# Query and key stacks of three narrow attentions: six copies in DRAM and one load each, in place of three parts and six loads

## What is computed

```python
Q = (queries @ W_q.T).reshape(b, lq, H, DH).transpose(2, 0, 1, 3)
K = (keys @ W_k.T).reshape(b, lk, H, DH).transpose(2, 0, 1, 3)
V = (keys @ W_v.T).reshape(b, lk, H, DH).transpose(2, 0, 1, 3)
scores = jnp.einsum('hbqd,hbkd->hbqk', Q, K) / jnp.sqrt(jnp.float32(DH))
scores = jnp.where(key_mask[None, :, None, :], scores, NEG)
attn = jax.nn.softmax(scores, axis=-1)
out = jnp.einsum('hbqk,hbkd->hbqd', attn, V)
...
x = x + _L0_xattn_ref(_layernorm(x, axis=-1), ctx_1024, _lenS2, L0_xattn_W_q, ...)
x = x + _L0_ffn_ref(_layernorm(x, axis=-1), ...)
```

## Time and profile before

| | |
|---|---|
| median of three runs | 909.4 us (902.32 to 909.76) |
| the profiled execution, its own time | 903.74 us |
| its span, first to last instruction | 902.0 us |
| TensorE busy | 741.0 us, 82% |
| VectorE busy | 482.6 us, 54% |
| ScalarE busy | 374.1 us, 41% |
| mean granted TensorE clock | 0.913 of full speed |
| DMA | 77.49 MB, mean 86 GB/s |

### The profile page before, as it was taken

The page is one execution under the profiler, slowest core; times in us unless marked ns, Lnnn a source line. Parts: engine busy times, 40 slices in busy tenths (PEclk is TensorE's granted clock), DMA queues, the critical chain, the costliest instruction groups (busy, mean ns, idle before and its releaser), DMA issues. The chain is left out here.

```text
span 902.0 us, 14540 instructions
## 1 busy us (share of the span) xinstructions
PE 741.0 (82%) x5219; PEld 571.3 (63%) x5219; DVE 482.6 (54%) x1477; ACT 374.1 (41%) x768; POOL 136.5 (15%) x282
## 2 busy tenths in 40 slices
PE   3158899999997999889399928799899997697367
PEld 2025588788774666679388825476798994354266
DVE  6345674354234567875945317566544536576423
ACT  1015664244333555553154404366433432466234
POOL 7011130000000001001800001111100001112224
PEclk9558999999998999999799969899999998899679
DMA  4729940002145554994002540432000531432153
GB/s 120 135 41 265 160 105 1 1 1 72 47 140 151 182 157 140 196 194 81 1 1 57 62 57 7 80 101 75 2 1 36 67 59 19 81 103 79 48 167 147
DMA packets 78164, 77.49 MB, mean 86 GB/s; under 512 B 10849, under 2 KB 69237, under 8 KB 78094
## 3 DMA queue, kind: packets, MB, share of 16 engines
q1 hardware_dynamic: 77230, 74.99, 38.1%
q0 software_dynamic: 864, 1.58, 0.5%
HBM read 46.65 MB, written 28.78 MB: 84 GB/s over the span
## 5 line engine op out<-in xcount | busy, mean ns | idle before, releaser
L1703 PEld LDWEIGHTS bank<-W,late 128*128 128x128 f32 x1600 | 185.8, 192 | 8.3 <-issue 3.8
L1703 PE MATMUL bank<-W,late 128*128 128x128 f32 x1600 | 186.5, 275 | 0.0
L988 DVE SCALAR_TENSOR_TENSOR x_res<-bank,comb,x_res 128x128 f32<-128x128 f32 x200 | 56.3, 345 | 168.1 <-PE bank L1703 166.4
L1277 ACT ACTIVATE late<-bank,b 128x512 f32<-128x512 f32 x136 | 91.8, 688 | 95.2 <-PE bank L1435 94.1
L753 DVE TENSOR_REDUCE negmax<-bank 128x2 f32<-128x512 f32 x128 | 85.2, 689 | 79.3 <-PE bank L1471 51.2
L1471 PE MATMUL bank<-big 128*128 128x256 bf16 x320 | 71.8, 300 | 63.8 <-DMA big<-parts_scratch 53.2
L1206 ACT ACTIVATE late<-bank 128x512 f32<-128x512 f32 x120 | 70.8, 595 | 64.2 <-PE bank L1511 29.8
L1435 PE MATMUL bank<-nH,wH 128*128 128x512 f32 x200 | 89.0, 445 | 2.5 <-DVE nL L791 2.4
L1471 PEld LDWEIGHTS bank<-big 128*128 128x128 bf16 x320 | 27.7, 104 | 93.8 <-issue 50.6
L1435 PE MATMUL bank<-nL,wH 128*128 128x512 f32 x200 | 81.1, 405 | 0.0
L1435 PE MATMUL bank<-nH,wL 128*128 128x512 f32 x200 | 80.9, 404 | 0.0
(11 more groups left out here) (269 smaller groups left out, 1293.7 us busy)
## 6 DMA issues: line engine op xcount, KB each, us to landing
W<-in_f_w SPq DMA_DIRECT2D x50, 256.0 KB, 4.3
rows_scratch<-zrow SPq DMA_DIRECT2D x1, 9252.0 KB, 56.7
late<-bands_scratch SPq DMA_DIRECT2D x8, 1024.0 KB, 5.8
big<-parts_scratch SPq DMA_DIRECT2D x18, 256.0 KB
big<-parts_scratch SPq DMA_DIRECT2D x36, 128.0 KB
W<-in_f_wx SPq DMA_DIRECT2D x8, 512.0 KB, 3.9
big<-in_f_wx SPq DMA_DIRECT2D x7, 578.0 KB, 6.7
bands_scratch<-late SPq DMA_DIRECT2D x3, 1276.0 KB, 6.4
```

The costliest lines, as they stand in the source:

```text
L988: ins = v.scalar_tensor_tensor(x[:, t, :], bank[4 + u % 2][:, 128 * i:128 * (i + 1)], comb[:, t, e:e + 1], x[:, t, :], ALU.mult, ALU.add)
L1277: ins = a.activation(dst, bank[c][:, :], func, bias=b1[:, bi, FC * e + c:FC * e + c + 1])
L1703: ins = mm(dst[:, 128 * i:128 * (i + 1)], hid[u % 2][:, c, 128 * i:128 * (i + 1)], W[:, e, F + 128 * c:F + 128 * (c + 1)], start=c == 0, s ...
```

## The change

The parts are stored six times, once for each pair, in an order in which each run of equal or neighbouring parts is one DMA (`RUNS`: three copies, two, one). The scratch tensor is pair, partition, token. The columns of the query and key weights (and the biases of a3) are reordered before the kernel, so that the projection leaves value i of head h on partition i*H + h. Then pair and i run together along the scratch, and a stack is one load over 96 or 48 partitions. The pairs themselves are the same, in another order. The second half of the queries in a2 and a3 is loaded whole behind group 4. `st.w` counts 48 for a stack in place of 16, `st.k` and `st.q` 16 in place of 96.

```diff
-PAIRS = ((0, 0), (0, 1), (1, 0), (1, 1), (0, 2), (2, 0))
+PAIRS = ((0, 0), (0, 1), (0, 2), (1, 0), (1, 1), (2, 0))
+RUNS = (((0, 3, 0), (3, 2, 1), (5, 1, 2)), ((0, 3, None), (3, 2, None), (5, 1, 0)))
...
-        scratch = nc.dram_tensor("parts_scratch", [2, 128, 3, TOK], bf16, kind="Internal").ap()
+        scratch = nc.dram_tensor("parts_scratch", [2, len(PAIRS), 128, TOK], bf16, kind="Internal").ap()
...
-                sp.dma_start(scratch[side, :, :, cols], parts[:, :, cols]).then_inc(sem("st.w"), 16)
-
-            def stack_in(key, side, half=None, pairs=range(len(PAIRS))):
+                for first, n, part in RUNS[side]:
+                    src = parts[:, 0:n, cols] if part is None else parts[:, part:part + 1, cols].broadcast_to([128, n, cols.stop - cols.start])
+                    sp.dma_start(scratch[side, first:first + n, :, cols].rearrange("r p t -> p r t"), src).then_inc(sem("st.w"), 16)
+
+            def stack_in(key, side, half=None):
...
-                sp.wait_ge(sem("st.w"), 16 * (3 * LAYER_OF[key] + (1 if side else 2 + half)))
-                src = scratch[side].rearrange("(h i) c t -> i h c t", i=d)
-                for r in pairs:
-                    pair = PAIRS[r]
-                    sp.dma_start(dst[r * d:(r + 1) * d, 0:H, cols], src[:, :, pair[side], cols])\
-                      .then_inc(sem("st.k" if side else f"st.q{half}"), 16)
+                sp.wait_ge(sem("st.w"), 48 * (3 * LAYER_OF[key] + (1 if side else 2 + half)))
+                src = scratch[side].rearrange("r (i h) t -> (r i) h t", h=H)
+                sp.dma_start(dst[0:len(PAIRS) * d, 0:H, cols], src[:, :, cols]).then_inc(sem("st.k" if side else f"st.q{half}"), 16)
...
                     if g == 4:
-                        stack_in(key, 0, 1, range(2))
-                    if g == 5:
-                        stack_in(key, 0, 1, range(2, 6))
+                        stack_in(key, 0, 1)
...
-                dve.wait_ge(sem("st.w"), 16 * (3 * LAYER_OF[key] + 1))
+                dve.wait_ge(sem("st.w"), 48 * (3 * LAYER_OF[key] + 1))
...
-                pe.wait_ge(sem("st.k"), 16 * len(PAIRS) * (LAYER_OF[key] + 1))
+                pe.wait_ge(sem("st.k"), 16 * (LAYER_OF[key] + 1))
...
-                        pe.wait_ge(sem(f"st.q{b // 2}"), 16 * len(PAIRS) * (LAYER_OF[key] + 1))
+                        pe.wait_ge(sem(f"st.q{b // 2}"), 16 * (LAYER_OF[key] + 1))
...
-        aw += [T(g[n + s]) for s in "qkvo"]
+    by_row = {n: np.arange(D).reshape(h, D // h).T.reshape(-1) for n, h in (("L0_xattn_W_", 8), ("L2_xattn_w_", 16), ("L3_xattn_W", 16))}
+    for n, order in by_row.items():
+        aw += [T(g[n + s])[:, order] if s in "qk" else T(g[n + s]) for s in "qkvo"]
```

More of the change, by code:

```diff
@@ L499, in row_numbers @@
                 pool.wait_ge(*at("f1", "acc", 16))
-                pool.wait_ge(sem("st.w"), 16 * 9)
+                pool.wait_ge(sem("st.w"), 48 * 9)
                 for hf in range(2):
@@ L675, in keys_parts @@
                 if n:
-                    dve.wait_ge(sem("st.w"), 16 * 3 * n)
+                    dve.wait_ge(sem("st.w"), 48 * 3 * n)
                 split(KT, slice(0, TOK), "kp")
@@ L1868 @@
     aw = []
-    for n in ("L0_xattn_W_", "L2_xattn_w_", "L3_xattn_W"):
-        aw += [T(g[n + s]) for s in "qkvo"]
+    by_row = {n: np.arange(D).reshape(h, D // h).T.reshape(-1) for n, h in (("L0_xattn_W_", 8), ("L2_xattn_w_", 16), ("L3_xattn_W", 16))}
+    for n, order in by_row.items():
+        aw += [T(g[n + s])[:, order] if s in "qk" else T(g[n + s]) for s in "qkvo"]
     a = {
@@ L1875 @@
         "aw": np.stack(aw),
-        "qkb": T(np.stack([g["L3_xattn_bq"], g["L3_xattn_bk"]])),
+        "qkb": T(np.stack([g["L3_xattn_bq"], g["L3_xattn_bk"]])[:, by_row["L3_xattn_W"]]),
         "rows": np.stack([g["L1_ffn_g1"], g["L1_ffn_be1"], g["L1_ffn_mix_b"], g["L1_ffn_g2"], g["L1_ffn_be2"],
```

## The result

| | before | after |
|---|---|---|
| median | 905.94 us (902.32 to 909.76, 4 runs) | 873.07 us (871.91 to 875.55, 4 runs) |
| ratio | | 0.964, 95% interval 0.958 to 0.970 |
| span of the profiled execution | 902.0 us | 873.8 us |
| mean granted TensorE clock | 0.913 | 0.924 |

What follows compares the result with a forecast made beforehand. TensorE, busy 741.0 of 902.0 us, idled 53.2 us on late stack loads to few partitions. Six waits saving 39.6 us plus 3 of clock gave 861 from the profile, 867 from the median; forecast 864, range 850 to 884.

Steps and rivals of the forecast that it cites:

- a2, first half, 15.6 us: First scores of a2: query store goes at 510.5, load ready at 520.6, so the whole 15.6 us wait goes.
- a2, second half, 5.6: Scores of a2's second query half: store-to-scores path shorter by 7.2 us, so the 5.59 us wait is covered.
- a3, first half, 2.0: First scores of a3: path falls from 14.7 to 10.1 us, so the whole 1.97 us wait goes.
- rival 2: a2's own rows are slow by themselves; if their 26.2 us stay, 7.7 us of wait stay: 872 us. Chance 12%.
- my cover of 3 us: a2, first half: load ready at 520.6, TensorE comes at 523.8, so the wait is covered by 3 us.
- a0, first half, 8.5 us: First scores of a0 start at 42.5 us in place of 51.06, with the key data taking 4.7 us.
- a0, second half, 1.9 us: Second-half scores of a0: store-and-load path 8.8 us, so 1.9 us of the 2.54 us wait go.
- a3, second half, 6.0 us: Second-half scores of a3: 6.0 of 6.70 us go; 0.7 stay for group 5's maxima rows behind the load.
- The clock, 3 us: Both attentions a2 and a3: less time at TensorE's half clock gives back 3 us, bounds 0 and 5.
- my own signs of being wrong: Load window staying at 125 or 65 GB/s, own rows still 26 us, or new `nmT` wait above 1 us in a2/a3.
- rival 1: Number of DMA engines, not partitions, sets the load rate: 125 GB/s, waits fall 22.6 us, 879 to 885, say 882. Chance 13%.
- Rival 3: Slower: a load uses few engines or ports, runs at 65 GB/s while stores carry double; 31 us lost, 935. Chance 3%.

Runs made afterwards that it cites:

- run 1: Changed kernel plus thirteen loads behind its last store, to measure rates: 16, 32, 48, 64, 96, 128 partitions took 4.6, 6.0, 12.6, 11.3, 15.0, 11.2 us.
- run 7: Changed kernel with a0's key load in two token halves, the second behind the first queries: 868.30 us, ratio 0.962, against the changed kernel's 869.53.
- runs 5 and 6: Changed kernel, a2 and a3's second query half loaded behind group 5's maxima row (877.36 us, 0.969), or half ahead, half behind (867.31 us, 0.960).

## Why the prediction was right, and by how much it was off

The direction and the order of size were right, and the cause in the main: 864 forecast, 873.07 measured (869.53 and 869.79 later), within 850 to 884. Of 45 us that 864 promised on 909.4, 33 came on 905.9. Term by term, each against the rows after:

- **a2, first half, 15.6 us; a2, second half, 5.6; a3, first half, 2.0.** All three went whole. The own rows, rival 2, need 14.64 us and not 26.20, and end about when the key load does, so they were slow mostly because it was; the store is issued at 506.96, where the split ends. But the whole 15.6 us came by luck in the margin. The key data took 12.8 us where I had 8.3, and in the second profile a half took 8.9 us from its load to the scores (507.45 to 516.34) where I had 6.1. At that pace the load issued at 510.74 is ready near 519.6 (an estimate), and TensorE comes at 520.06: of my cover of 3 us 0.4 is left. In the second profile it was not enough:

```profile
516.34 0.27 PE L1469 MATMUL bank<-big 128*128 128x256 bf16 x1 [0.37 <-DMA big<-parts_scratch]
```

- **a0, first half, 8.5 us: 4.6 came.** The key store was right (5.55 against 5.3). The step that failed is the rate over 96 partitions. I put them near the 128 of the weights, 332 GB/s and 4.7 us; they took 7.4 us, 213 GB/s, and run 1 has 210 for this count. That delays the query store behind them by the 2.9 us that run 7 took back, and the query load by another 1.0 (5.84 against 4.8).
- **a0, second half, 1.9 us: the wait grew by 1.8.** The path from the split to the scores was 60.44 to 71.30, 10.9 us, where I had 8.8 and the old kernel 10.7. The store was right (3.7), the load of 7.2 us was not (4.8). 1.0 of the 2.4 us is the rate, as in the first half; the rest I had no term for, and no run isolates it. It comes where the weights of f0 are issued right behind the load, from 64.73 us on. And TensorE came to it earlier than before, 20.5 us after the first scores in place of 22.1, which turns into wait. In the second and third profile it was 2.11 and 4.50 us.
- **a3, second half, 6.0 us: 3.6 came** (6.70 + 0.32 before, 3.38 after; 4.8 and 4.9 in the two later profiles). That the row of group 5 would be late behind the load was foreseen, and runs 5 and 6 show it; its size was not 0.7 us. The step is again a rate: the middle of 125 and 261 GB/s for 48 partitions was a guess between ends, and the truth was the low end, 123 to 127.
- **The clock, 3 us.** The mean rose from 0.913 to 0.924 in the first profile, but TensorE's busy time did not fall (741.0 and 741.3) and the span is shorter by no more than the waits, so there the clock gave nothing that shows. In the later profiles, at 0.935 and 0.933, it was 735.2 and 736.3. That spread is larger than the term, so it can't be told apart.

Sum of the waits: 39.6 forecast, 29.5 measured. Two of my own signs of being wrong came: a load window near 125 GB/s (a2), and a wait above 1 us for `nmT` rows (a3). For the 48 partitions of a2 and a3 rival 1 was right, in the rate and in the reason: the load went from 65 to 123 GB/s because sixteen engines work at 8 GB/s each in place of eight, and by run 1 a load over 16 partitions (114 GB/s) would have been nearly as good as one over 48 (no kernel with such loads was run). It fails as a rule for other counts, as 32 and 128 partitions show, and for the 96 of a0, where its 125 was too low. In a0 the cause is the one that I gave, more partitions in a load, but at two thirds of the rate that I gave it (213 for 332 GB/s). The time landed between its 882 and my 864, as the rates do. The estimate from the Trainium skill that stood beside the sum (SBUF — State Buffer, Door 1: The DMA port swizzle), 4.8 us for the data of a half, was nearer than my 4.1; the last window after the change has 5.8. Rival 3, a slower kernel, needed loads at under 90 GB/s; run 3, with the loads cut as before, was slower, by 2.0% at 923 us where it had 935.

## What to carry to other kernels

The time of a DMA into SBUF depends on how many partitions its destination has, and not only on its size: here, with 32 KB for each, 48 partitions took longer than 64 or 128, and 32 half of that. Ask first how many of the sixteen DMA engines a load keeps busy (the DMA share tells), then how long one partition holds an engine. Measure the rate for the exact count of partitions, since between two known counts it doesn't run in a straight line. And a long load in a shared queue is paid twice: whatever small transfer is issued behind it, a store or a row of maxima, lands when the load has; cutting two such loads at the place where their first part is needed gave 5.3 us on top of the change.

## What was not expected of the hardware

A load of 32 KB for each partition took 6.0 us for 32 partitions, 12.6 for 48, 11.3 for 64, 16.0 for 112 and 11.2 for 128: fewer partitions and bytes can take longer. Two loads to partitions 0 to 47 and 64 to 111, issued together, took 24.5 us, nearly twice the 12.6 of one. Two profiles of one kernel, with granted clocks of 0.924 and 0.935, differ by 6.1 us in TensorE's busy time, also in a stretch that the stacks do not touch.
